# A gated cross-attention and sign-weight feed-forward kernel: every woven item gets a slot of its own in a written-out table

## The reference, cut to what matters

```
x = x + tanh(g_xattn) * (attention(layernorm(x) @ Wq + bq, ctx @ Wk + bk, ctx @ Wv + bv) @ Wo + bo)
x = x + tanh(g_ffn) * ffn(layernorm(x))
ffn(h): h = concat(h, -h); h = 2*relu(s0 * h @ sign(k0)); h = 2*relu(s1 * h @ sign(k1)); return s2 * h @ sign(k2)
```

## Time and profile before

| | us |
|---|---|
| time, median of 3 runs | 1641.92 (1639.31 to 1643.83) |
| the profiled execution's own time | 1646.27 |
| its span, from first to last instruction | 1644.5 |
| PE busy, PEld busy | 1529.3 (93%), 1391.9 (85%) |
| DVE, ACT, POOL busy | 1160.8 (71%), 774.1 (47%), 155.5 (9%) |
| mean granted TensorE clock | 0.979 of full speed |

### The profile page before, as it was taken

One profiled execution on the slowest core, in us unless ns is written; L12 is line 12 of the kernel. 1 busy time (PEld: TensorE's weight loads), 2 busy tenths in 40 slices (PEclk: granted clock), 3 DMA queues, 4 the chain that ended last, 5 costly groups with the idle time before them and its releaser, 6 DMA issues.

```text
span 1644.5 us, 48200 instructions
## 1 busy us (share of the span) xinstructions
PE 1529.3 (93%) x20568; PEld 1391.9 (85%) x20568; DVE 1160.8 (71%) x2289; ACT 774.1 (47%) x1684; POOL 155.5 (9%) x273
## 2 busy tenths in 40 slices
PE   6799888999999899999989999899999989999999
PEld 4587787988989788898989889798898978889897
DVE  5878678777667677776777667677776777677653
ACT  3442543635546364553635445364553635446331
POOL 2102011010100101010010100101010010100100
PEclk9999999999999999999999999999999999999999
DMA  8543232331414324143432524223142433413100
GB/s 243 116 91 59 53 84 53 93 68 46 107 33 105 59 63 88 43 95 65 98 66 50 101 40 98 59 69 82 43 95 53 98 65 60 91 41 97 33 28 15
DMA packets 283062, 121.09 MB, mean 74 GB/s; under 512 B 249696, under 2 KB 265056, under 8 KB 282848
## 3 DMA queue, kind: packets, MB, share of 16 engines
q1 hardware_dynamic: 280784, 117.48, 33.5%
q10 hardware_dynamic: 2064, 0.53, 0.1%
HBM read 37.76 MB, written 16.78 MB: 33 GB/s over the span
## 4 chain that ended last, share of the span: by engine, by line
PE 58%; DVE 21%; ACT 8%; issue 7%; DMA 4%; POOL 2%; SPq 0%; DVEq 0%; ACTq 0%; POOLq 0%
PE bank L1450 12%; PE bank L1451 12%; PE bank L1476 7%; PE bank L1416 6%; PE bank L1417 6%; ACT Pf L619 3%; DVE h L991 3%; DMA PT<-Phl 2%; DVE nmax L921 2%; DVE Phl L925 2%; PE bank L1333 2%; PE bank L1334 2%; PE bank L1335 2%; DVE Fp L976 2%; PE bank L1317 2%
## 5 line engine op out<-in xcount | busy, mean ns | idle before, releaser
L1450 PE MATMUL bank<-H,W 128*128 128x128 f16 x6720 | 805.0, 223 | 46.5 <-ACT C L714 43.9
L1451 PE MATMUL bank<-H,W 128*128 128x128 f16 x6720 | 804.7, 223 | 0.0
L1450 PEld LDWEIGHTS bank<-H,W 128*128 128x128 fp8e5 x6720 | 668.7, 100 | 54.3 <-ACT C L714 46.1
L1451 PEld LDWEIGHTS bank<-H,W 128*128 128x128 fp8e5 x6720 | 670.8, 100 | 2.9
L1416 PE MATMUL bank<-hT,W 128*128 128x256 f16 x1024 | 228.6, 273 | 2.3 <-DVE hT L861 1.9
L1417 PE MATMUL bank<-hT,W 128*128 128x256 f16 x1024 | 228.6, 273 | 0.0
L1476 PE MATMUL bank<-W,h 128*128 128x256 fp8e5 x1624 | 208.1, 273 | 16.8 <-DVE h L991 15.6
L961 DVE TENSOR_TENSOR C<-bank,C 128x256 f32<-128x256 f32 x240 | 101.2, 422 | 170.6 <-PE bank L1451 91.6
L1476 PEld LDWEIGHTS bank<-W,h 128*128 128x128 f16 x1624 | 153.4, 98 | 38.3 <-issue 17.8
L619 ACT ACTIVATE Pf<-bank,nmax 128x128 f32<-128x128 f32 x496 | 141.0, 369 | 75.0 <-DVE nmax L921 75.0
L566 POOL TENSOR_TENSOR xn<-pvs 128x128 f32<-128x128 f32 x120 | 65.4, 545 | 1112.7 <-DVE pvs L934 1112.7
(11 more groups left out here) (150 smaller groups left out, 2031.2 us busy)
## 6 DMA issues: line engine op xcount, KB each, us to landing
Qst<-q_bounce SPq DMA_DIRECT2D x120, 128.0 KB, 2.8
Y<-in_x_dram SPq DMA_DIRECT2D x16, 512.0 KB, 3.7
R<-X SPq DMA_DIRECT2D x16, 512.0 KB, 3.2
q_bounce<-Qhl SPq DMA_DIRECT2D x120, 64.0 KB
out_dram<-R SPq DMA_DIRECT2D x15, 512.0 KB, 3.5
W<-in_L_ffn_k_dram SPq DMA_DIRECT2D x10, 512.0 KB, 7.1
W<-in_L_ffn_k_dram SPq DMA_DIRECT2D x2, 1024.0 KB, 18.6
PT<-Phl SPq DMA_TRANSPOSE x120, 3.1
```

Source lines behind the costliest of these rows:

```text
L1450: mm(o, w, H0[:, 0, i, b_of, :], start=first, stop=False, skip_group_check=True)
L1451: last = mm(o, w, H0[:, 1, i, b_of, :], start=False, stop=i == PAIRS - 1, skip_group_check=True)
```

## The change

The places are no longer made by `weave`. Two tables, `WEAVE_0` (chunk 0) and `WEAVE` (all others), give each item a slot and a place within the slot.

1. Items are cut finer. `CT`, `T1`, `T2` keep ACT's high part; DVE's low part and SP's transposition are items of their own, `CTL`, `T1L`, `T2L`. DVE's low part of the queries is `QD`, apart from `Q`.
2. The group work becomes items: `RE` (`rectify`, with a group and 0 to 3), `GS` (`group_sums`), `GT` (`group_last`), `GH` (`group_hi`), `GL` (`group_lo`). `take` and `add` stay in `feed`. What group 3 has left no longer stands at slot 0 of the next chunk, but at slots 48 and 49 of its own; `group_hi` 0 stands behind the fourth `rectify` there.
3. Items of the attention stand at other slots: for example `Q` at 2, 4, 9, 12 (before 1, 3, 7, 11), `PS` at 13, 16, 18, 21, 23, 25, 27, 29 (before 13, 16, 19, 21, 23, 25, 27, 29), `PV` at 18, 20, 22, 25, 28, 29, 31, 34 (before 17, 20, 23, 25, 27, 29, 31, 33), `WO` at 38 and 40 (before 37 and 39).
4. The three PSUM banks of `Q`, `S`, `PV`, `WO` follow the new order, and PE's wait for a bank's last user is found in the order of chunk 0 or of the others.
5. `WO` writes its statistics to a buffer of its own, `stats2`. `N1` of a later chunk waits until `T2L` has read `xn`.

No instruction on tiles is added or left out, and none changes its shape. The core of the diff:

```diff
-            put(slot + 1, "EX", u)
-            put(slot + 2, "PS", u)
...
-            put(normalised + t, "LN", t, 2)
-            put(normalised + 2 + t, "N1", t, 2)
-            put(normalised + 3 + t, "T1", t, 2)
...
-    WEAVE = weave((11, 14, 17, 19, 21, 23, 25, 27), (17, 20, 23, 25, 27, 29, 31, 33), (32, 34), 37, 36, 40)
...
+    WEAVE = {
+        2: [(1, ("Q", 0)), (1, ("QD", 0))],
+        3: [(1, ("QS", 0))],
+        4: [(1, ("Q", 1)), (1, ("QS", 1)), (1, ("QD", 1))],
+        5: [(1, ("QL", 0))],
+        6: [(1, ("QL", 1))],
+        9: [(1, ("Q", 2)), (1, ("QS", 2)), (1, ("QD", 2))],
+        10: [(1, ("S", 0))],
+        12: [(1, ("Q", 3)), (1, ("EX", 0))],
+        13: [(1, ("S", 1)), (1, ("PS", 0)), (1, ("QS", 3))],
+        15: [(1, ("EX", 1)), (1, ("QD", 3))],
+        16: [(0, ("RE", (0, 0))), (1, ("PS", 1))],
+        17: [(1, ("QL", 2)), (1, ("S", 2))],
+        18: [(1, ("EX", 2)), (1, ("PV", 0)), (1, ("S", 3)), (1, ("PS", 2))],
+        20: [(0, ("RE", (0, 1))), (1, ("EX", 3)), (1, ("PV", 1))],
+        21: [(0, ("GS", (0,))), (0, ("RE", (0, 2))), (0, ("GH", (0, 0))), (0, ("RE", (0, 3))), (1, ("QL", 3)),
+            (1, ("S", 4)), (1, ("PS", 3))],
+        22: [(0, ("GT", (0,))), (0, ("GH", (0, 1))), (1, ("EX", 4)), (1, ("PV", 2)), (1, ("S", 5))],
+        23: [(0, ("RE", (1, 0))), (0, ("GL", (0, 0))), (1, ("PS", 4)), (0, ("GL", (0, 1)))],
+        24: [(1, ("EX", 5))],
+        25: [(1, ("PS", 5)), (1, ("PV", 3)), (1, ("S", 6))],
+        26: [(1, ("EX", 6)), (1, ("S", 7))],
+        27: [(0, ("RE", (1, 1))), (1, ("PS", 6)), (0, ("GS", (1,)))],
+        28: [(0, ("RE", (1, 2))), (0, ("GH", (1, 0))), (0, ("RE", (1, 3))), (1, ("EX", 7)), (1, ("PV", 4))],
+        29: [(0, ("GH", (1, 1))), (0, ("GL", (1, 0))), (0, ("GT", (1,))), (1, ("PS", 7)), (1, ("PV", 5))],
+        30: [(0, ("RE", (2, 0))), (0, ("GL", (1, 1)))],
+        31: [(1, ("PV", 6))],
+        34: [(1, ("CT", 0)), (1, ("CTL", 0)), (1, ("PV", 7))],
+        35: [(1, ("CT", 1)), (1, ("CTL", 1))],
+        38: [(0, ("RE", (2, 1))), (1, ("LOAD", 0)), (1, ("WO", 0))],
+        39: [(0, ("GS", (2,)))],
+        40: [(1, ("N2", 0)), (1, ("WO", 1)), (2, ("LN", 0))],
+        41: [(0, ("RE", (2, 2))), (0, ("RE", (2, 3))), (2, ("LN", 1)), (1, ("T2", 0)), (1, ("T2L", 0)),
+            (1, ("N2", 1))],
+        42: [(0, ("GT", (2,))), (1, ("T2", 1)), (2, ("N1", 0))],
+        43: [(0, ("GH", (2, 0))), (0, ("GH", (2, 1))), (1, ("T2L", 1)), (2, ("N1", 1)), (2, ("T1", 0))],
+        44: [(0, ("GL", (2, 0))), (2, ("T1L", 0)), (0, ("GL", (2, 1)))],
+        45: [(2, ("T1", 1)), (2, ("T1L", 1))],
+        46: [(0, ("RE", (3, 0)))],
+        48: [(0, ("RE", (3, 1))), (0, ("GS", (3,)))],
+        49: [(0, ("RE", (3, 2))), (0, ("RE", (3, 3))), (0, ("GT", (3,))), (0, ("GH", (3, 0))),
+            (0, ("GH", (3, 1))), (0, ("GL", (3, 0))), (0, ("GL", (3, 1)))],
+    }
...
+        def there(ahead, item):
+            if ahead <= 0:
+                return f + ahead >= 1 and (item[0] == "RE" or not late(f + ahead, item[1][0]))
+            return f + ahead < CHUNKS and (item[0] != "LOAD" or f + 2 < CHUNKS)
...
-                if kind in CUT and not first:
+                if kind in ("CTL", "T1L", "T2L"):
...
-                if kind == ("QD" if first else "Q"):
+                if kind == "QD":
...
-                    V_.bn_stats(stats[:, n, :], X[:, n, :]).then_inc(wo_step, 1)
+                    V_.bn_stats(stats2[:, n, :], X[:, n, :]).then_inc(wo_step, 1)
...
-                        if n == 3 and not late(f, n - 1):
-                            group_hi(n - 1, f, 0)
-                        if n > 0 and not late(f, n - 1):
-                            group_hi(n - 1, f, 1)
```

More of the change, by code:

```diff
@@ L138, in gated_block_kernel, with late @@
-    QUERIES_0[0] = [(1, (kind, t)) for kind in ("N1", "T1") for t in range(TT)]
-    LOOP_ITEMS = [item for where in (QUERIES, WEAVE) for slot in sorted(where) for _, item in where[slot]]
-    def woven(s, f):
[L143 to L146, removed]
+    def late(f, q):
+        return f == CHUNKS - 1 and q >= GROUPS // 2
@@ new lines, in gated_block_kernel @@
+    WEAVE = {
[41 rows of a table added]
+    }
+    ORDER_0, ORDER = ([item for slot in sorted(where) for ahead, item in where[slot] if ahead == 1]
+                      for where in (WEAVE_0, WEAVE))
+    def woven(s, f):
+        def there(ahead, item):
+            if ahead <= 0:
+                return f + ahead >= 1 and (item[0] == "RE" or not late(f + ahead, item[1][0]))
+            return f + ahead < CHUNKS and (item[0] != "LOAD" or f + 2 < CHUNKS)
+        return [(ahead, item) for ahead, item in (WEAVE if f else WEAVE_0).get(s, []) if there(ahead, item)]
@@ L697, in attend @@
                         .then_inc(p_hi, 1)
+                if kind == "RE":
+                    rectify(*n, a)
+                if kind == "GH":
+                    group_hi(*n, a)
             def pair_hi(i, f):
@@ L721, in rectify, with group_hi @@
                                          source, ACT.Relu).then_inc(h1_hi, 1)
[L722 to L726, removed]
+                    return
+                if n == 0 and q == 0:
+                    act.wait_ge(l0_lo, nth(f, NP, NP - 1))
+                if n == 0 and q > 0:
+                    act.wait_ge(h2_lo, 2 * group(f, q) - 1)
+                if n == 3 and group(f, q) > 0:
+                    act.wait_ge(h2_lo, 2 * group(f, q))
+                row = 1 + (H_R11, H_R22, -1, H_R21)[n]
+                nc.scalar.activation(Fp[:, 1:3, row, :], source, ACT.Relu).then_inc(h2_relu if n < 3 else l1_copy, 1)
+            def group_hi(q, n, f):
                 rows = (EARLY_ROWS, LATE_ROWS)[n]
@@ L791, in feed @@
                         take(n, s, f, C22)
[L792 to L799, removed]
-                        act.wait_ge(l1_done, nth(f, NL1, 7 * n + s))
-                        rectify(n, f, 3, H_R21 + 1, halves_of(ROLES[n][A]))
             for a, item in FIRST:
@@ L944, in attend @@
                     dve.wait_ge(x1_ready, nth(a, NT, n))
[L945 removed]
+                    V_.bn_stats(stats2[:, n, :], X[:, n, :]).then_inc(wo_step, 1)
                     wait_apart(dve, wo_step, nth(a, NT, n))
[L947 removed]
+                    V_.bn_aggr(mv2[:, n, :], stats2[:, n, :]).then_inc(wo_mv, 1)
+                if kind == "GS":
+                    group_sums(*n, a)
+                if kind == "GT":
+                    group_last(*n, a)
+                if kind == "GL":
+                    group_lo(*n, a)
                 if kind == "N2":
@@ L1019, in feed @@
                 if kind == "L0":
-                    if n == 0 and f > 1:
-                        group_last(GROUPS - 1, f - 1)
-                        group_lo(GROUPS - 1, f - 1, 0)
-                        group_lo(GROUPS - 1, f - 1, 1)
                     if f:
@@ L1052, in feed @@
                     banks_of = ROLES[n]
-                    if s == P1 and n > 0 and not late(f, n - 1):
-                        group_last(n - 1, f)
-                        if n != 3:
-                            group_lo(n - 1, f, 0)
                     if s == P2:
@@ L1059, in feed @@
                         add(n, s, f, C11, banks_of[B])
-                        if n == 3 and not late(f, n - 1):
-                            group_lo(n - 1, f, 0)
-                        if n > 0 and not late(f, n - 1):
-                            group_lo(n - 1, f, 1)
                     if s == P6 and late(f, n):
@@ L1079, in feed @@
                         last_rest(n, 3, banks[banks_of[A]][:, 0:CHUNK].rearrange("p (j n) -> p j n", j=2))
-                    if s == P4 and not late(f, n):
-                        group_sums(n, f)
             def finish(f):
```

104 lines of the change are left out of this document (45 added, 59 removed), and 25 rows, old and new, of the table WEAVE_0.

## The result

The changed kernel takes **1529.29 us** (median of 4 runs, 1528.94 to 1529.56) against 1640.78 us for the one before (median of 4, 1639.31 to 1643.83, the three runs of the table above among them): a ratio of 0.9318 with a 95% interval of 0.9302 to 0.9334, or 111.5 us less. The forecast was 1550 us, with a range of 1536 to 1582.

A forecast was written before the change was run, and what follows sets the result against it. PE bounds the kernel: a chunk's 98.43 us is 90.91 matmuls, 2.14 half-rate and 5.38 idle. Savings of 84.4 (chunks 2 to 13) + 9 + 2 = 95.4 us gave 1550.9 profiled, predicted 1550 us, range 1536 to 1582.

The forecast's parts named there:

- the knot (slots 41 to 47): End of chunks 2 to 13: reordered ACT and DVE queues end PE's waits for `take` at P7, saving 40.1 us.
- slot 43's `take` behind `T2` 1: At P6 of group 3: `take` is ready 5.7 us after the projection, P6 due at about 6.1, margin 0.4 us.
- rival (b): The stall moves to slot 45, P6 waiting for `take` behind `T2` 1: at 2.5 us late, 1588 us; chance 0.14.
- the clock: Chunks 2 to 13: half-rate time of 2.14 us a chunk, 25.7 us in all, goes with the 3 us stall.
- Chunk 1: Two long stalls, 3.8 and 3.2 us, and 3 us of half-rate time go, 1 given back: 9 us, bounds 4 and 15.
- The floor of a chunk: Chunks 2 to 13: matmuls at full clock take 90.91 us a chunk, read from chunk 14's PE busy time.
- Late transfers: Chunks 2 to 13: 0.5 us a chunk kept for transposed probabilities that land late, from 6.4 us of waits.
- Chunks 0, 14, 15: Outer chunks: chunk 14 saves 1.0 us, chunks 0 and 15 save 1.0 us together.
- (d): The walk is too pessimistic: nothing left in chunks 2 to 13, chunk 1 gives 15 us; 1538 us or just under, chance 0.07.
- (c): The clock falls anyway, half-rate time stays: 1550 + 26 = 1576 us, chance 0.05.
- (e): ACT and DVE block at another slot of group 3, the 3.34 us stay: about 1630 us, chance 0.02.
- (f): Slower: the softmax chain becomes the bound and `PV` waits; 1700 us at 1.5 us per `PV`, chance 0.05.

The follow-up runs named there:

- new_end: The order of before in the changed kernel's code, with the new order in slots 41 to 49 alone: 1575.34 us, ratio 0.9597.
- old_end: The changed kernel with the old order in slots 42 to 46 alone: 1583.08 us, ratio 0.9645.
- the two experiments: extra2 and extra4, the changed kernel with added DVE reductions ahead of `LN` 1: 1536.95 us and 1556.05 us.
- late_low: The changed kernel with `GS` of group 1 moved from slot 27 to 28 and `GT` ahead of `GL` at slot 29: 1558.01 us, ratio 0.9492.
- old_zero: The changed kernel with the order of before in chunk 0 alone: 1532.31 us, ratio 0.934.
- extra4: The changed kernel with four unread reductions of 512 columns ahead of `LN` 1 in DVE's queue, chunks 1 to 13: 1556.05 us, ratio 0.9486.
- extra2: The changed kernel with two unread reductions of 512 columns ahead of `LN` 1 in DVE's queue, chunks 1 to 13: 1536.95 us, ratio 0.9372.
- old_table: The changed kernel's code, fine items and `stats2` kept, with a table that writes out the order of before: 1645.55 us, ratio 1.0024.

## Why the prediction was right, and where it fell short

**Right, the knot (slots 41 to 47).** The 40.1 us at `take` are gone; new_end shows that the end of the chunk does it alone, old_end that without it 32.5 us stay. The place foreseen as thinnest, slot 43's `take` behind `T2` 1, is the thinnest of the three places followed for chunks 2 to 13: 0.63 us read and 0.57 by the two experiments, against 0.4; then come the low half with 0.67 (0.8 foreseen) and P7 with 0.80 (1.3 foreseen). The transpositions for `PV` have less, since PE waits for two of them. My walk put the end of that `take` 5.7 us after the projection and it comes after 5.4 (1157.17 less 1151.77). late_low shows what it costs when the low half comes late. One sentence of rival (b) does not fit its own sum: 1 us of delay costs 0.6 us only for the first, each further one costs all of it, as its 2.1 us for 2.5 has it.

**Right, the clock, though it was tied too closely to the stall.** It went to 1.00 with the stalls, and new_end, with no wait above 1.84 us in chunks 2 to 13, has 1.00 there too. But "0.98 where PE stalls for 3 us" is a mean over chunks: two of the twelve, chunk 11 of the earlier trace rows among them, had the stall and kept the full clock (last section). The Trainium skill, "TensorE: Matmul & The Clock Gate", section "What's actually happening", says that the clock is throttled by default and that activity releases it. The traces agree in one direction only: from chunk 1 to chunk 14, each half-rate stretch of the ten traces follows a wait of PE of 2.0 us or more, but not each such wait is followed by one. The forecast's 2.14 us a chunk of half-rate time held some 0.35 that was not: in the two chunks with the stall and the full clock PE is busy for 91.26 us and not for 90.91.

**Wrong, the sum: 21.6 us of span too little.** The path was right and the sizes were not: four terms of the sum were put too small. (The forecast's own last step, too, does not come out: 1550.9 less half of the 4.4 us is 1548.7, and it says 1550.)

*Chunk 1, 9 counted, 18.5 measured (9.5 of the miss).* I took the two long stalls and 3 of the 5.7 us of half-rate time, and gave 1 back for its fuller DVE queue. Nearly all of it went: idle time fell from 15.6 to 94.60 - 92.35 = 2.25 us, 13.3 less, and busy time by 5.2 us (97.53 to 92.35). One of its three half-rate stretches had followed the 2.0 us wait for exponentials, which was no part of my count. My upper bound of 15 was no bound, since it took the idle time alone and left out the half-rate time beside it. The small waits that I left to chunk 1 went with the long ones: three waits stay, of 1.2, 0.7 and 0.3 us.

*The floor of a chunk, 90.91 taken, 90.42 measured (12 x 0.49 = 5.9).* I read the time of the matmuls from chunk 14's busy time. But chunk 14 had three waits (1.04, 0.31 and 0.05 us), 1.39 us of idle time in all, and lasted 92.30 - 90.42 = 1.88 more than a chunk without any. When PE has to wait, the record of the last matmul before the wait counts as busy to its end (it lasts 0.22 us, where a successor starts after 0.056). In the experiments a recorded wait of 0.45 us makes a chunk 0.63 longer (91.05), one of 1.64 us 1.81 longer (92.23), one of 1.70 us 1.86 (92.28), where 90.42 is the chunk without waits: 0.16 to 0.18 more than the wait, each time. A floor has to be read from a stretch without waits, or corrected by 0.17 for each.

*Late transfers, 6.0 us kept, 2.2 left (3.8).* Three of the eight `PV` have a slot more behind their `PS`, and the order in SP's queue is another; the seven waits for PT became two, of 0.5 us together, and one of 0.7 for xT; with the drains and what else stands in chunks 2 to 13 above 12 x 90.42 = 1085.04 this makes 2.2. Which of the moved entries did it was not tried.

*Chunks 0, 14, 15 (2.0 counted, 5.8 measured; 3.8), and 1.3 lost ahead of chunk 0.* Chunk 0 had 1.9 us of waits for exponentials and 0.8 for a load of Q, both gone. I had not read its waits. With the old order there alone it lasts 2.4 us longer again (old_zero).

The sum of the four is 9.5 + 5.9 + 3.8 + 3.8 - 1.3 = 21.7, the 21.6 but for rounding. **The range failed with two of them:** its low end was that of (d), which rested on the same 90.91 and on the bound of 15 for chunk 1. With 90.42 and 18.5 in their places (d) would have been 1538 - 5.9 - 3.5, some 1529.

**The rivals.** (b) was not met. extra4, which is (b) with DVE 2.38 us late, costs 1.81 us a chunk; the 1.1 us of half-rate time that I had put on top of the stall is not in it. (c) falls with the clock of 1.00. (e) falls with the `take` for which PE no longer waits, (f) with the waits at `PV`: 0.5 us for PT in 96 of them. (d) was nearest: the walk was too pessimistic.

What stays open is why some transpositions land late, what decides whether a long wait brings half-rate time, and the 1.3 us ahead of chunk 0: that stretch lasts 73.5 to 75.7 us over these kernels (73.5 in extra2, whose table is that of the changed kernel with its 74.9), so the change is not seen in it.

## What to carry to other kernels

Where two engines each run an order written out by hand, look for the instruction that waits at the head of one queue while what the critical engine wants stands behind it; the cure is a place in a list and cost nothing here. To forecast it, follow each queue against the engine that never stops and note the margin of each place, and do this for the odd chunks (the first, the fullest) by themselves, since that is where the margins are least and the gain may be largest. Take the floor from a stretch in which the bounding engine has no wait; when you bound a gain, add the half-rate time to the idle time; and check a rule such as "the clock falls with the stall" chunk by chunk, not on a mean.

## What the hardware showed that I had not expected

The half-rate time does not follow a stall one for one. In the kernel before, two of the twelve chunks stalled at `take` and kept the full clock: chunk 4 (3.28 us) and chunk 11 (3.36 us), the one of the earlier trace rows. Chunk 8 (3.64 us) did not:

```profile
478.40:575.60 97.20, 91.28 (x1308) 84.29 (x1306) 69.57 (x141) 48.90 (x106) 8.82 (x16) 1.00 0.36 72
870.90:970.10 99.20, 93.92 (x1308) 86.93 (x1306) 69.93 (x141) 48.89 (x106) 8.81 (x16) 0.97 0.38 71
```

old_table has one such chunk too, with 3.65 us. In chunks 2 to 13 of the experiments, waits of 1.64 to 1.99 us (extra4) and of 1.70 (late_low) never brought half-rate time; one of 2.06 in late_low did (the window of chunk 4 above: clock 0.98, busy time 92.24 for 90.60); of the eight chunks of old_end whose wait was 2.29 to 2.31 five had it and three had not, with the same instructions, and its four with 2.7 us or more all had it. A single stretch cost 1.6 us in most chunks (94.5 - 92.9; 1.4 in one), and in five chunks of the kernel before it was twice as long and cost 2.6 (93.92 less 91.28). So the same order can cost nothing, 1.6 or 2.6 us a chunk on top of its stall, and in a forecast that is a mean and not a price for each chunk.

A profile without any idle time on PE is also possible: in chunk 9 PE is busy for 90.40 of 90.40 us while weights are loaded for 84.28 of them, DVE works for 76% of the time, and DMA engines for 39%.
